# A window-attention stack's value copies, let go in four groups instead of one burst per tile

## The reference, cut to what matters

```python
def local_attention(q, k, v):
    ...
    def look(t):
        p = jnp.pad(t, ((0, 0), (0, 0), (1, 0), (0, 0), (0, 0)))
        return jnp.concatenate([p[:, :, :nw], p[:, :, 1:]], axis=3)
    bk2, bv2 = (look(bk), look(bv))
    ...
    sim = jnp.einsum('bhwie,bhwje->bhwij', bq, bk2) * QK_SCALE
    sim = jnp.where(mask, -jnp.finfo(sim.dtype).max, sim)
    attn = jax.nn.softmax(sim, -1)
    out = jnp.einsum('bhwij,bhwje->bhwie', attn, bv2)
...
for i in range(DEPTH):
    x = attn_layer(shift_tokens(x), Wqkv[i], q_scale[i], k_scale[i], Wo[i]) + x
    x = ffn_layer(shift_tokens(x), ln_g[i], ln_b[i], W1[i], b1[i], W2[i], b2[i]) + x
```

## Time and profile before

| | |
|---|---|
| Time, median of 3 runs | 1877.75 us (1877.37 to 1881.33) |
| The profiled execution's own time | 1872.37 us |
| Its span | 1870.6 us |
| Busy: PE / DVE / ACT / POOL | 84% / 65% / 53% / 43% |
| The 48 tiles of the stack | about 520 to 1395 us of the span |
| Value copies | 744 of 64 KB, all on SP's queue |

### The profile page before, as it was taken

One profiled execution on the slowest core, in us unless ns is written; L12 is line 12 of the kernel. 1 busy time (PEld: TensorE's weight loads), 2 busy tenths in 40 slices (PEclk: granted clock), 3 DMA queues, 4 the chain that ended last, 5 costly groups with the idle time before them and its releaser, 6 DMA issues. The chain is left out here.

```text
span 1870.6 us, 42756 instructions
## 1 busy us (share of the span) xinstructions
PE 1570.2 (84%) x17249; PEld 1060.8 (57%) x17249; DVE 1223.7 (65%) x2351; ACT 990.5 (53%) x1861; POOL 797.4 (43%) x1098
## 2 busy tenths in 40 slices
PE   3005376997778999989999999999878999999999
PEld 2002154675536566666666666666655776676676
DVE  6846674214777887878888888887854666665211
ACT  1033143333445666756666666666655776776332
POOL 0000070101766676776776776776631333333000
PEclk8556677999989999999999999999998999999899
DMA  3000002010133323313422322422220000000111
GB/s 113 15 10 1 3 1 64 23 34 15 37 88 82 102 56 82 102 46 76 107 56 75 100 65 69 107 63 52 62 70 1 1 1 1 1 1 1 35 35 34
DMA packets 74573, 88.25 MB, mean 47 GB/s; under 512 B 22994, under 2 KB 42936, under 8 KB 74346
## 3 DMA queue, kind: packets, MB, share of 16 engines
q1 hardware_dynamic: 73562, 85.28, 17.5%
q10 hardware_dynamic: 816, 0.24, 0.1%
HBM read 35.21 MB, written 2.34 MB: 20 GB/s over the span
## 5 line engine op out<-in xcount | busy, mean ns | idle before, releaser
L1511 POOL TENSOR_TENSOR st_r<-st_r,st_t 128x512 f32<-128x512 f32 x192 | 244.0, 1276 | 189.3 <-DVE st_t L1477 189.3
L1433 PE MATMUL PS<-st_wqkv,st_xs 128*128 128x512 f32 x576 | 301.9, 609 | 16.5 <-DVE st_t L1477 8.6
L2288 POOL TENSOR_SCALAR la_p<-la_p,la_rden 128x589 f32<-128x589 f32 x64 | 112.9, 1764 | 230.7 <-DVE la_rden L2307 230.7
L1528 POOL TENSOR_TENSOR st_r<-st_r,st_gy 128x512 f32<-128x512 f32 x192 | 195.8, 1052 | 3.8
L1469 DVE TENSOR_TENSOR st_r<-PS,st_rot 128x512 f32<-128x512 f32 x192 | 129.1, 672 | 99.0 <-ACT st_sqh L1453 98.4
L1212 ACT ACTIVATE m_h<-PS 128x512 f32<-128x512 f32 x128 | 76.5, 598 | 142.3 <-PE PS L1144 142.3
L2301 DVE TENSOR_REDUCE la_nmx<-PS 128x1 f32<-128x589 f32 x128 | 92.7, 766 | 84.4 <-PE PS L2146 84.4
L1453 ACT ACTIVATE st_sqh<-PS 128x512 f32<-128x512 f32 x192 | 114.5, 596 | 53.5 <-PE PS L1433 52.2
L808 POOL MEMSET l_s<- 128x192 f32 x2 | 0.5, 260 | 331.6 <-DVE x L649 218.2
L2253 ACT ACTIVATE la_p<-PS,la_nmx 128x589 f32<-128x589 f32 x128 | 95.1, 748 | 82.1 <-DVE la_nmx L2301 82.0
L1237 DVE SCALAR_TENSOR_TENSOR m_y<-PS,m_g,m_y 128x128 f32<-128x128 f32 x112 | 31.5, 344 | 159.7 <-PE PS L1153 159.7
(11 more groups left out here) (311 smaller groups left out, 3432.4 us busy)
## 6 DMA issues: line engine op xcount, KB each, us to landing
st_vv<-st_v SPq DMA_DIRECT2D x744, 64.0 KB, 2.0
st_wqkv<-in_st_wqkv SPq DMA_DIRECT2D x18, 512.0 KB, 4.3
m_w<-in_m_w SPq DMA_DIRECT2D x32, 256.0 KB, 3.1
st_wo<-in_st_wo SPq DMA_DIRECT2D x6, 512.0 KB
st_w<-in_st_w SPq DMA_DIRECT2D x6, 341.0 KB
la_wc<-in_la_wc SPq DMA_DIRECT2D x1, 1344.0 KB, 7.1
ca_blocks<-in_blank SPq DMA_DIRECT2D x1, 1280.0 KB, 6.9
st_qks<-in_st_qks SPq DMA_DIRECT2D x6, 128.0 KB, 4.0
```

The source lines that it names most:

```text
L1433: pe.matmul(PS[:, 2 + m % 2, :], self.xs[:, b, P * t:P * t + P], self.wqkv[:, l % 2, k, 512 * half:512 * half + 512], start=True, stop=Tru ...
L1511: pool.tensor_tensor(r, r, self.t2[:, c % 2, :], ALU.add).then_inc(self.added, 1)
L1528: pool.tensor_tensor(r, r, y[:, 8 * c:8 * c + 8].unsqueeze(2).broadcast_to([P, 8, D2]), ALU.mult)\
L2288: pool.tensor_scalar(self.p[:, v % 2, 0, :], self.p[:, v % 2, 0, :], self.rden[:, v % 4, 0:1], None, ALU.mult).then_inc(self.scaled0, 1)
```

## The change

The first group of copies goes out as before. The other three first wait on `qk_used`: for the last part (c = 3) of the same tile, then for parts 0 and 1 of the next tile. The bound 4N serves the last tile, which has no next one. The copies, their number, their order and their semaphores stay.

```diff
             if t > 0:
                 for e in range(2):
                     self.v_copy(sp, T, e, 0, 0, self.v_crossed[T % 2])
-            for e in range(2):
-                for w in range(4):
+            for k in range(4):
+                e, half = divmod(k, 2)
+                if k:
+                    sp.wait_ge(self.qk_used, min(4 * T + 3 + k, 4 * self.N))
+                for w in (2 * half, 2 * half + 1):
                     self.v_copy(sp, T, e, 1, w, self.vshift[t])
                     if w:
                         self.v_copy(sp, T, e, 0, w, self.vshift[t])
```

## The result

The changed kernel takes 1897.03 us in the median of 8 runs (1890.46 to 1901.96), the kernel before 1879.54 us beside it. The ratio is 1.0086, 95% interval 1.0069 to 1.0103: slower by about 16 us. The forecast was 1879.2 us and no change, with a range up to 1884. It missed on the slow side.

What follows compares the result with a forecast made beforehand. No single engine fills the span (TensorE 84%) and the copies are hidden. 1872.37 us + 1.2 for late copies + 0.3 for single landings is 1873.9; the median, 5.38 higher, is 1879.2 (+0.08%, no change), range 1876 to 1884.

Steps and rivals of the forecast that it cites:

- the release: End of the L1477 that frees group 3, part 1 of the next tile; at t = 0 the evacuation follows 4.35 us later.
- 3.99 us needed at t = 3: Last own copies, next tile without crossed ones: needed 3.99 us behind the release against 4.13 available, so in time.
- 5.25 for the crossed copies at t = 0: Steps without a load: crossed copies land 5.25 us behind the release, against 5.77 that delays nothing; evacuation 0.9 later, inside idle time.
- The rest: Added SP waits, loads moving about half a step, and the last tile's `la_wc` pushed to 1377: nothing costed.
- the 1.1 us: Lateness over 5.77 us with a load in front, steps 4, 12, 20, 28, 36; said to vanish in 4 and 28.
- left the clock out: Upper clock level (2.4 GHz) taken as granted nearly throughout; copies are no work for TensorE, so no clock effect was priced.
- The weight load in front of the crossed copies: 512 KB load_w delays crossed copies to 6.9 us (5.87 if they pass it); cost 1.2 us, at most 3.3.
- the steps with t = 1: Step 21's kind: 7.90 us of room behind the release, 5.25 needed, or 6.9 with a load; in time.
- Rival 1: Slower by the tail of six copies, if landings take 3.7 us: 13.2 us, 1891; chance 0.18.
- Rival 2: Faster by quieter scores, if copies' traffic causes TensorE's 8 stalls without a releaser: up to 15.6 us, 1862; chance 0.07.
- The last line of the forecast: Wrong if L1446 starts a delay seen in the next scores, without a load, or the scores' stalls change in number.
- Rival 3: Change hardly does what it says: at t = 3, 13 copies go in a row; forecast's time, chance 0.75 together with it.

Runs made afterwards that it cites:

- experiment 5: The changed kernel with each weight load issued behind group 1 of its tile, away from the scores; 1.0005 of the kernel before.
- Experiment 6: The kernel before, single bursts kept, with only the weight loads moved behind the first six copies of the next tile's burst; 1.0083 of the kernel before.
- experiment 9: The kernel before with loads moved into the next burst, each 512 KB load_w as four of 128 KB behind copies 6, 8, 10 and 12; 1.0034.
- experiment 3: The changed kernel with each weight load issued just behind the next tile's two crossed copies instead of in front; 1.0060 of the kernel before.

## Why the prediction was wrong

**Right.** That the copies are hidden, and when they go out: the release, 3.99 us needed at t = 3 (3.82 to 3.85 measured in steps 7 to 39, and the evacuation there unchanged to 0.01 us), 5.25 for the crossed copies at t = 0 (5.13 in steps 8 to 40 without a load), the evacuation 0.9 us later with the idle time of the L1670 shorter by as much, nothing left of it by the next mix. In experiment 5 the whole of this was run alone, and it gave the forecast's "no change".

**The step that failed: "The rest".** It says "The loads themselves move by about half a step and are wanted a step or more later", and on that the move of the loads was costed at nothing. The sentence is true: no row of after shows anyone waiting for the weights. But it asks only who reads the loaded bytes. It doesn't ask what else uses the 16 DMA engines while the load runs. Before, the load went out behind the scores (1030.69 against 1025.74). After, it goes out just ahead of them, and one of the 138 blocks of TensorE's program is there 3.7 us later than it was (6.07 us behind the start of the scores, not 2.33). Experiment 6 moves the loads and nothing else and costs 0.83%, about the whole slowdown; experiment 5 keeps the groups, moves the loads away from the scores, and is at 1.0005; experiment 9 cuts them into quarters and takes more than half of the 0.83% back. This is the step that made the time come out slower than forecast.

Two more places of the prediction go with it. It let the 1.1 us vanish in the stalls of steps 4 and 28, and took these as they were; they grew from 2.14 to 3.70 and from 1.70 to 3.66 us, and the steps are 3.83 and 3.59 us longer. And it left the clock out because the copies are no work for TensorE; the clock fell behind the longer stalls, and TensorE's matmuls in the stack took 12.6 us more (791.4 to 804.1).

**Its second part was a size.** "The weight load in front of the crossed copies" had the right mechanism and the right end of its bounds: the copies don't pass the load. The forecast was 6.9 us behind the release; 7.4 to 9.1 was measured (7.58 in step 20). The 6.9 rests on the landing of one load, 3.8 us. The page of before has 4.3 as the median of such loads, with which the same sum gives 7.6:

```profile
st_wqkv<-in_st_wqkv SPq DMA_DIRECT2D x18, 512.0 KB, 4.3
```

I also let the idle times behind it take 0.7 of it. In steps 12, 20 and 36 the mixes come 1.05, 1.66 and 2.52 us later, 5.2 us together, where 1.2 stood in the sum and 3.3 was its upper bound. The same 6.9 was taken for the steps with t = 1, "in time" against 7.90; there 7.3 to 8.6 was measured, beyond the 7.90 in steps 13 and 37 (+1.37 and +0.65 us). By the ratio of experiment 3 this part is about 0.26 of the 0.86%, with intervals that overlap. The rule of the Trainium skill that was cited, "DMA: Bandwidth & Descriptors", section "Queues, rings and completion order", agrees with the trace: at 7.4 us and more the copies didn't pass the load (passing it would have given 5.87).

**Rival 1** had the sign and about the size (1891 us), by another mechanism: it wanted landings of 3.7 us in steps without a load, and those steps (8, 24, 32) are unchanged to 0.02 us. That its side came out was luck: the chance of 0.18 that it carried wasn't earned by it.

**Rival 2** said that the stalls without a releaser come from traffic, and set against it that they are in few steps while the bursts are in all. That they hang on traffic is right, but on a large load's and not on 64 KB copies': without the bursts (experiment 5) the longest stall is 2.6 us as in before, and nothing is gained. The rows for the true cause were in hand: 8 stalls, 15.6 us, and one of 2.16 in step 16, with no releaser. I read them only for what could be gained and not for what could make them longer. The last line of the forecast named them as the sign of being wrong, without a price.

**Rival 3** held in part: behind each release SP goes through its copies in a row, and the waits are there in number without cost.

**What stays open.** Each row here is from one execution, and which blocks of the program meet the scores differs between the traces: steps 17, 29 and 44 move by 2.4 to 3.4 us each with no load of their own to explain it, and whether the groups have a part in it no run settles. That a 512 KB load holds the block back is read from their times in the traces; what in the DMA engines does it isn't there. How long the fetch of the program had been asked for before its packet ran isn't in the trace, so its delay is read from when it ran before and after. That the lower clock follows from TensorE's idle time is read from their order in time; for stalls near 2.2 us it isn't regular: before has 2.16 us at 831.55 with the clock at 1, and experiment 5 has 2.20 us at 855.01 with a lower stretch of 3.4 us from 856.5.

## What to carry to other kernels

When a change moves a DMA, or a wait ahead of one, ask for each large transfer behind it on the queue what else is using the DMA engines in its new place: small copies that are issued behind it, and the engines' own programs. Here TensorE's stalls "<- issue" of a microsecond or more, which stood at mostly the same steps in every trace, were program fetches with no slack; look for the packets of the "instruction" queue just ahead of their ends, and keep loads of hundreds of KB out of the microseconds ahead of them, or spread them in pieces. Don't price a step from one trace of before: the loss in step 29 looked like the load's and was there without it. And price each moved load by experiment or by bounds, also where its reader has a whole step to spare.

## What the runs showed of the hardware

- TensorE's program came over the kernel's own DMA engines in blocks of 16 KB (138 packets, 35345 instructions). With a 512 KB load issued 0.9 and 0.6 us ahead of the scores, one block ran 4.8 and 5.5 us behind their start instead of about 1, and the stall grew from 1.66 to 5.51 and 6.05 us. With the load in quarters of 128 KB, one of them ahead of the scores, it was 2.7 us at that place.
- All 126 stalls without a releaser of over 0.9 us in TensorE's matmuls, in twelve traces, ended 1.1 to 1.7 us behind the end of such a block's packet.
- 64 KB copies issued right behind a 512 KB load landed up to 4.9 us after their issue in the changed kernel, against 2.0 undisturbed.
- In step 27 of the changed kernel, after 3.1 us without work, TensorE's granted clock was 0.50 (1.2 GHz) for 6.8 us, and in it sixteen matmuls took 3.27 us in place of 1.95.
